# A graph network's attention sums: one gathered tile in 48 fetched by SyncE row by row, and ScalarE waiting for the gathers itself

## The reference

```python
h = (x @ W).reshape(num_nodes, H, C)
a_src = (h * att_src).sum(-1)
a_dst = (h * att_dst).sum(-1)
e = jax.nn.leaky_relu(a_src[src] + a_dst[dst], 0.2)
m = jax.ops.segment_max(e, dst, num_segments=num_nodes)
ex = jnp.exp(e - m[dst])
denom = jax.ops.segment_sum(ex, dst, num_segments=num_nodes)
alpha = ex / denom[dst]
out = jax.ops.segment_sum(alpha[:, :, None] * h[src], dst, num_segments=num_nodes)
return out.reshape(num_nodes, H * C) + bias
```

## Time and profile before

| | us |
|---|---|
| three executions | 9349.14, 9346.64, 9349.06 (median 9349.06) |
| the profiled execution | 9349.14 |
| its span, first to last instruction | 9347.4 |
| first attention sum, first gather to last | 5371.4 to 6618.9 |
| second attention sum, first gather to last | 6704.9 to 7950.9 |

### The profile page before, as it was taken

How to read it: one execution, slowest core, us unless ns; L and a number is a source line. 1 busy time by engine, 2 the same in 40 slices (tenths; PEclk the granted TensorE clock), 3 DMA queues, 4 the chain that set the end, 5 groups by cost and what they waited for, 6 DMA issues and landing times. The chain is left out here.

```text
span 9347.4 us, 179303 instructions
## 1 busy us (share of the span) xinstructions
PE 7186.3 (77%) x38061; PEld 4861.1 (52%) x38181; DVE 6015.8 (64%) x20921; ACT 3122.2 (33%) x10511; POOL 6584.5 (70%) x6970
## 2 busy tenths in 40 slices
PE   6555547888796788877788767777577777799999
PEld 4222224343343444333333356666466666799999
DVE  6666655444444444456655567777577777799888
ACT  2222210000030000000000145555455555699998
POOL 3777777777716777767777677777577777477776
PEclk5555556666796666679988877777777777899999
DMA  5222224222253222222222122222222222212111
GB/s 124 85 89 84 89 80 96 55 55 55 54 242 85 55 55 55 54 55 55 54 54 54 52 60 60 60 60 60 50 60 60 60 60 60 83 53 53 53 53 51
DMA packets 312751, 637.84 MB, mean 68 GB/s; under 512 B 138402, under 2 KB 181541, under 8 KB 300200
## 3 DMA queue, kind: packets, MB, share of 16 engines
q0 software_dynamic: 222080, 416.54, 18.2%
q1 hardware_dynamic: 81444, 212.40, 6.8%
q10 hardware_dynamic: 8484, 1.48, 0.1%
HBM read 479.02 MB, written 150.90 MB: 67 GB/s over the span
## 5 line engine op out<-in xcount | busy, mean ns | idle before, releaser
L1193 POOL DMA_INDIRECT relsum_rows<-relation_table,tab_idx x1950 | 1840.4, 944 | 824.4 <-issue 398.7
L1252 PE MATMUL relsum_sums<-relsum_hot,relsum_rows 128*128 128x128 f32 x3900 | 1311.4, 433 | 516.1 <-DMA relsum_rows<-relation_table,tab_idx 457.2
L1252 PEld LDWEIGHTS relsum_sums<-relsum_hot,relsum_rows 128*128 128x128 f32 x3900 | 883.4, 274 | 1456.9 <-DMA relsum_rows<-relation_table,tab_idx 1409.0
L1057 POOL DMA_INDIRECT conv_rows<-tensor_table,src_idx x997 | 941.9, 945 | 406.9 <-issue 227.3
L1193 POOL DMA_INDIRECT gcnsum_rows<-x_table,src_idx x985 | 933.4, 948 | 329.9 <-issue 183.6
L1057 POOL DMA_INDIRECT gat1sum_rows<-gat_table,src_idx x997 | 944.9, 948 | 303.8 <-issue 231.6
L1057 POOL DMA_INDIRECT gat2sum_rows<-gat_table,src_idx x997 | 943.3, 946 | 303.8 <-issue 232.2
L717 POOL DMA_INDIRECT records<-sort_recs,place_rows x968 | 926.8, 957 | 295.2 <-issue 295.2
L1205 DVE TENSOR_SCALAR relsum_hot<-relsum_digits,dst_rel,w 128x128 f32<-128x128 f32 x1994 | 806.5, 405 | 421.4 <-issue 420.1
L1255 PE MATMUL relsum_streamed<-relsum_wide 128*128 128x512 bf16 x1874 | 1033.2, 551 | 0.0
L2253 ACT ACTIVATE conv_rows_attr<-conv_rows,conv_rec 128x64 f32<-128x64 f32 x2991 | 754.1, 333 | 51.3 <-SPq L2212 36.1
(11 more groups left out here) (418 smaller groups left out, 16108.7 us busy)
## 6 DMA issues: line engine op xcount, KB each, us to landing
relation_table<-table_row SPq DMA_DIRECT2D x30, 2048.0 KB, 6.3
relsum_rows_SP<-relation_table SPq DMA_DIRECT2D x2816, 0.5 KB
relsum_rows_ACT<-relation_table ACTq DMA_DIRECT2D x2816, 0.5 KB
relation_table<-sort_space SPq DMA_DIRECT2D x40, 1024.0 KB
relsum_rows<-relation_table,tab_idx POOLq DMA_INDIRECT x1950
place_lo_wide<-lo_rows SPq DMA_DIRECT2D x121, 256.0 KB
gcnsum_rows_SP<-x_table SPq DMA_DIRECT2D x1536, 0.5 KB
relation_table<-place_extra SPq DMA_DIRECT2D x20, 1024.0 KB
```

The costliest lines, as they stand in the source:

```text
L1057: pool.indirect_dma_start(bufs[:, t % depth, :], None, table, bass.IndirectOffsetOnAxis(ap=idx[:, t:t + 1], axis=0)).then_inc(landed[t % l ...
L1193: pool.indirect_dma_start(rows[:, t % depth, :], None, table, bass.IndirectOffsetOnAxis(ap=idx[:, t:t + 1], axis=0)).then_inc(landed[t % d ...
L1252: pe.matmul(bank[:, 0:P], tile_rows, hot[:, t % HOTS, :], start=True, stop=True).then_inc(s["multiplied"], 1)
```

## The change

In the attention sums, tiles 46, 94, ... 958 (buffer 46 of 48, one in each of the 20 rounds) are left out of GpSimd's queue. SyncE no longer relays arrivals. It writes the 20 lists of byte offsets to DRAM, and in each round reads one list back, waits until the one side buffer is free, and issues 128 DMAs of 576 bytes. ACT waits for the `landed` semaphores of the gathers itself, up to four for a turn. Once in a round, between turns 2 and 3 of the round's first group, it waits for the side tile, copies it (128x144) into buffer 46 and waits for its own copy. DVE makes the byte offsets in one instruction at the start.

```diff
--- before.py
+++ after.py
@@ -1047,11 +1047,13 @@
 
 
 
-def gather_rows(pool, env, table, idx, bufs, landed, free, free_at, count=TILES):
+def gather_rows(pool, env, table, idx, bufs, landed, free, free_at, count=TILES, aside=()):
 
 
     depth = bufs.shape[1]
     for t in range(count):
+        if t in aside:
+            continue
         if t >= depth:
             pool.wait_ge(free, free_at(t - depth + 1))
         pool.indirect_dma_start(bufs[:, t % depth, :], None, table,
@@ -1710,7 +1712,7 @@
         fold_ps, spread_ps, factor_ps = (small_ps[:, k * SLOT_BUFS:(k + 1) * SLOT_BUFS] for k in range(3))
         sums = [ps(f"sums{j}", [P, 2, 256], F32) for j in range(3)]
         landed = [env.sig(f"landed{k}") for k in range(PHASES * SLOT_BUFS)]
-        names = ("arrived", "scores_staged", "turned", "kept", "ends_ready", "folded", "chained", "spread", "shifted",
+        names = ("scores_staged", "turned", "kept", "ends_ready", "folded", "chained", "spread", "shifted",
                  "exped", "p_turned", "p_ready", "wide_ready", "dist_ready", "hot_ready", "scaled_ready", "multiplied", "added")
         sig = {n: env.sig(f"attend_{n}") for n in names}
         s = {n: x.sem for n, x in sig.items()}
@@ -1720,6 +1722,15 @@
         first_wide = p_wide[:, 1, 0:FIRSTS, :].rearrange("p j (k h) -> p j k h", h=HEADS)
         firsts_ps = small_ps[:, 256:256 + HEADS * FIRSTS]
         firsts = {n: env.sig(f"first_{n}") for n in ("gathered", "spread", "turned")}
+        rounds = WHOLE // PHASES
+        side_buf = held - 2
+        side_tiles = range(side_buf, rounds * held, held)
+        side_row = 4 * width
+        side_rows = sb("side_rows", [P, width], F32)
+        side_bytes = sb("side_bytes", [P, rounds], I32)
+        side_numbers = sb("side_numbers", [1, P], I32)
+        side_listed = nc.dram_tensor(f"{tag}_side_listed", (rounds, P), I32, kind="Internal").ap()
+        side = {n: env.sig(f"{tag}_side_{n}").sem for n in ("listed", "list_out", "list_in", "landed", "kept", "begun")}
         block = ctx.enter_context(nc.Block(no_gpsimd_drain=True))
 
         def tiles_of(g):
@@ -1737,26 +1748,47 @@
                                         bass.IndirectOffsetOnAxis(ap=env.first_idx[:, j:j + 1], axis=0)
                                         ).then_inc(firsts["gathered"].sem, 16)
             gather_rows(pool, env, table, env.src_idx, rows, landed, s["multiplied"],
-                        lambda n: v["multiplied"](held + n), count=USED)
+                        lambda n: v["multiplied"](held + n), count=USED, aside=side_tiles)
 
         @block.sync
         def _(sp):
-            with sp.Fori(0, WHOLE // PHASES) as i:
-                for k in range(held):
-                    sp.wait_ge(landed[k].sem, i * 16 + landed[k].at(16))
-                    sp.sem_inc(s["arrived"], 1)
-            for k in range(USED - WHOLE * SLOT_BUFS):
-                sp.wait_ge(landed[k].sem, landed[k].at(16 * (WHOLE // PHASES + 1)))
-                sp.sem_inc(s["arrived"], 1)
+            sp.wait_ge(side["listed"], 1)
+            sp.dma_start(side_listed.rearrange("n p -> p n"), side_bytes[:, :],
+                         allow_slow_non_contiguous=True).then_inc(side["list_out"], 16)
+            sp.wait_ge(side["list_out"], 16)
+            table_bytes = table.bitcast(U8).rearrange("n f -> (n f)").rearrange("(o k) -> o k", o=1)
+            with sp.Fori(0, rounds) as i:
+                sp.dma_start(side_numbers[:, :], side_listed[bass.ds(i, 1), :]).then_inc(side["list_in"], 16)
+                sp.wait_ge(side["list_in"], i * 16 + 16)
+                sp.sem_inc(side["begun"], 1)
+                sp.wait_ge(side["kept"], i + 1)
+                sp.sem_inc(side["begun"], 1)
+                for c in range(0, P, RowByRow.AT_ONCE):
+                    numbers = nc.values_load_multi_w_load_instructions(
+                        side_numbers[:, c:c + RowByRow.AT_ONCE], engines=[ENGINES["SP"]], min_val=0,
+                        max_val=(table.shape[0] - 1) * side_row,
+                        skip_runtime_bounds_check_because="the records hold row numbers of the table")[1]
+                    for e in range(RowByRow.AT_ONCE):
+                        sp.dma_start(side_rows[c + e:c + e + 1, :].bitcast(U8),
+                                     table_bytes[:, bass.ds(numbers[e], side_row)]).then_inc(side["landed"], 16)
 
         @block.scalar
         def _(act):
-            def take_scores(g, f, turn):
+            def keep_side(i):
+                act.wait_ge(side["landed"], i * (16 * P) + 16 * P)
+                act.wait_ge(s["multiplied"], i * held + v["multiplied"](side_buf + 1))
+                act.copy(rows[:, side_buf, :], side_rows[:, :]).then_inc(side["kept"], 1)
+                act.wait_ge(side["kept"], i + 2)
+
+            def take_scores(g, f, turn, gathers):
                 four = slice(4 * turn, 4 * turn + 4)
                 bufs = slice(f * SLOT_BUFS + 4 * turn, f * SLOT_BUFS + 4 * turn + 4)
                 if turn == 0:
                     act.wait_ge(s["turned"], g + v["turned"](1))
-                act.wait_ge(s["arrived"], g * SLOT_BUFS + v["arrived"](min(4 * turn + 4, tiles_of(g))))
+                for k in range(4 * turn, min(4 * turn + 4, tiles_of(g))):
+                    buf = f * SLOT_BUFS + k
+                    if buf != side_buf:
+                        act.wait_ge(landed[buf].sem, gathers * 16 + landed[buf].at(16))
                 act.copy(scores[:, f, 0, four, :], rows[:, bufs, D:D + HEADS])
                 act.copy(scores[:, f, 1, four, :], rows[:, bufs, D + HEADS:width]).then_inc(s["scores_staged"], 1)
 
@@ -1791,21 +1823,25 @@
             for turn in range(2):
                 build(0, turn)
             stage_resets(0)
+            act.sem_inc(side["kept"], 1)
             for g in range(2):
                 for turn in range(4):
-                    take_scores(g, g, turn)
+                    take_scores(g, g, turn, 0)
             exponentials(0, 0)
             keep_numerators(0, 0)
             with act.Fori(0, WHOLE // PHASES) as i:
                 for f in range(PHASES):
                     g = i * PHASES + f
                     ahead, next_f = (f + 2) % PHASES, (f + 1) % PHASES
+                    gathers = i + (f + 2) // PHASES
                     build(g, 2)
-                    take_scores(g + 2, ahead, 0)
-                    take_scores(g + 2, ahead, 1)
+                    take_scores(g + 2, ahead, 0, gathers)
+                    take_scores(g + 2, ahead, 1, gathers)
                     build(g, 3)
-                    take_scores(g + 2, ahead, 2)
-                    take_scores(g + 2, ahead, 3)
+                    take_scores(g + 2, ahead, 2, gathers)
+                    if f == 0:
+                        keep_side(i)
+                    take_scores(g + 2, ahead, 3, gathers)
                     build(g, 4)
                     exponentials(g + 1, next_f)
                     keep_numerators(g + 1, next_f)
@@ -1815,7 +1851,7 @@
                 build(g, 2)
                 if f == 0:
                     for turn in turns_of(g + 2):
-                        take_scores(g + 2, 2, turn)
+                        take_scores(g + 2, 2, turn, rounds)
                 build(g, 3)
                 build(g, 4)
                 exponentials(g + 1, f + 1)
@@ -1873,6 +1909,8 @@
                     dve.drain()
                     dve.tensor_tensor(score[:, :], score[:, :], largest[:, :], ALU.subtract).then_inc(s["shifted"], 1)
 
+            dve.tensor_scalar(side_bytes[:, :], env.src_idx[:, side_buf:rounds * held:held], side_row, None,
+                              ALU.mult).then_inc(side["listed"], 1)
             dve.memset(acc[:, :, :], 0.0)
             dve.memset(factor[:, PHASES - 1, :], 0.0)
             if added_to_x is not None:
...
```

More of the change, by code:

```diff
@@ L1995, in attend @@
         turns = 4 * (USED_GRPS - 1) + len(turns_of(USED_GRPS - 1))
-        for n, count in (("arrived", USED), ("scores_staged", turns), ("turned", USED_GRPS + PHASES), ("kept", USED_GRPS + 1),
+        for n, count in (("scores_staged", turns), ("turned", USED_GRPS + PHASES), ("kept", USED_GRPS + 1),
                          ("ends_ready", USED_GRPS), ("folded", USED_GRPS), ("chained", USED_GRPS), ("spread", USED_GRPS),
@@ L2002, in attend @@
         for k in range(held):
-            landed[k].passed(16 * len(range(k, USED, held)))
+            if k != side_buf:
+                landed[k].passed(16 * len(range(k, USED, held)))
         for n, count in (("gathered", 16 * FIRSTS), ("spread", 1), ("turned", 1)):
```

## The result

| | us |
|---|---|
| kernel before, five executions | median 9348.3 |
| changed kernel, five executions | median 9299.45 (9297.75 to 9302.39) |
| ratio, 95% interval | 0.9949, 0.9938 to 0.9961 |
| span of the profiled execution | 9300.7 (before 9347.4) |

The change takes 48.9 us off, 0.5%. The forecast was 9299.0. Of all executions in this document one, of the last experiment with 16 more rows, took 10015 us at a granted clock of 0.58, and its time is left out.

A forecast was written before the change was run, and what follows sets the result against it. The prediction took GpSimd's own gather cadence, about 1.25 us, to bound the attention sums. Only the removed gathers counted, every other term being nothing: 9349.1 - 50.1 = 9299.0 us, range 9290 to 9335.

The forecast's parts named there:

- Gathers taken from GpSimd: GpSimd's queue in both attention sums: 20 gathers fewer in each, at 1.2525 and 1.2510 us, 50.1 us less.
- SyncE's rows at no cost to the cadence: Attention sums: GpSimd's gathers keep their cadence of about 1.25 us while SyncE fetches rows, so nothing is taken off.
- The fetch of 48.2 us, paced by its issue: SyncE's 128 row DMAs for a side tile: 48.2 us, set by the issuing engine and not by bytes.
- the rival by beats: Side tile's fetch: AXI beats of 576-byte rows set the pace, ring 81.7 us, kernel 10169; within 8 in 100 for slower.
- The ring of 53.4 us with 5.4 to spare: SyncE's one-buffer cycle of fetch 50.3, landing 2.5, copy and signals 0.6 us, inside a round of 58.8 us.
- the lower of the text's bounds: SyncE's one-buffer cycle at its shortest: 53.0 us, from a single fetch of 48.2 + 2.2 us.
- The first round: Start of the attention sums: first side tile lands near 5426.6, at worst 2 us late once; nothing taken.
- ACT's waits at nothing: ACT in the attention sums: 12 waits more in each group cost nothing; upper bound 0.1 us each, 3.6 a round.
- The followers' margin of 4.5 and 3.6 us: PE's waits for numerators in first and second sum: room in each round, against a round shortened by 1.25 us.
- the ring: Rival: SyncE's one-buffer cycle exceeds 58.8 us, each further microsecond costing 38; 8 in 100 slower, 4 in 100 mild.
- The followers' case: Rival: PE, DVE and ACT become the bound in the attention sums, up to 9355 us; 12 in 100.
- the change does nothing: Rival: something behind GpSimd, late DMA queues or a longer tail, takes the time again, 9349 us; 3 in 100.

The follow-up runs named there:

- the last experiment with 16 more rows: Changed kernel plus 16 more row DMAs each round and 48 idle increments ahead of SyncE's loop in the second sum, repeated: 49.1 us under the kernel before.

## Why the prediction was right

*Gathers taken from GpSimd* (50.1 us): 50.3 in the changed kernel's trace, 47.4 for 2 x 19 with no fetch at all. Right, cadence and count. That 9299.0 and 9299.45 lie within half a microsecond is luck: the five executions spread over 4.6 us, and 3.6 us of the gain in the trace were lost ahead of the sums and between them, a term that the text did not have.

*SyncE's rows at no cost to the cadence*: shown by fetching them beside. *The fetch of 48.2 us, paced by its issue*: 47.6 to 47.8, and 48.7 for the first. The 576 bytes and their place off a 256-byte boundary cost nothing that the issue does not hide; the rival by beats, 81.7 us, is excluded by this fetch.

*The ring of 53.4 us with 5.4 to spare*: it is 52.0 with 6.8, below the lower of the text's bounds. That bound is also added up wrongly: 48.2 + 2.2 and the 3.1 of landing, copy and signals are 53.5 and not 53.0. Two terms were off. Landing was taken from a list's read as 2.5 us and is 1.3. And the text said that the next list is in before the next copy; when the ring binds it is the other way round, and the list's read is on the path instead of the landing and the copy. Neither touched the time, since the room was not used up.

*The first round*: the list took 5377.31 - 5360.86 = 16.4 us to be written, between the 11.0 and the 18.4 of the text, and ACT waited 0.9 us for the first tile in the first sum, 3.4 in the second, and never again. Both are inside the buffers' 48 tiles, as forecast.

*ACT's waits at nothing*: right as far as 9 us can be told. *The followers' margin of 4.5 and 3.6 us*: enough, as forecast, and with six left out 5.6. PE's waits understate it; the follower that binds in the end is DVE, whose margin the text did not work out.

Of the rivals, the ring was the one to fear. With its room used up by 16 more rows, the place of a loop in memory cost 2.8 us of a round and some 27 us in one sum, and on one chip a ring of 83 us was the bound. Where the changed kernel was timed, its loop was not fetched anew, and its 6.8 us of room would have hidden the 2.8. The followers' case did not come up, and that the change does nothing is excluded by the times of the whole and of the first sum alone.

## What to carry to other kernels

When an engine issues at a fixed cadence and never waits by more than a fraction of a microsecond, a piece of its work is worth its cadence wherever it goes, as long as the others have the margin; read that margin from the waits of each of them, and test it by leaving more out: here 3.6 to 4.5 us were read and 5.6 found. Work moved to an idle engine through one buffer makes a ring: add up its whole cycle, next list and register loads included, set it against the round, and remember that past the round each microsecond costs once for every round. Leave some room in it: here the place of a loop took 2.8 us of a round, and one chip 31.

## What the runs showed of the hardware

The body of SyncE's loop was fetched anew in each round or not at all, depending on 48 instructions ahead of it: 173 against 92 instruction blocks of 8.2 KB in 1000 us, and 2.4 us more at the loop's edge. Row DMAs of 576 bytes issued by SyncE landed 1.2 to 1.3 us after the last issue. 128 of them took 47.6 us, and GpSimd's gathers beside them kept their 1.25 us. On one chip the median gather (947 ns) and the median row DMA of the attention sum (224 ns) were as fast as on the others, but some were held up: a gather took 1.488 us on average (1.19 times), a tile of row DMAs 79 us (1.66 times), and 16 row DMAs at a tile's end the usual 5.0 us.
